# A gated recurrence on one core: loads streamed four at a time, the last two gathers first, and a reordered first layer

## The chip, the cores and the metric

The kernel runs on one core of one Trainium2 chip. The metric is the device time of one execution in microseconds (us). Three runs of the kernel before gave 105.54, 105.76 and 106.26 us, median 105.76. The profiled execution took 106.02 us; the span of its instructions, on which all times of the trace are counted, is 104.2 us.

The engines are named as the profile names them: PE (TensorE, matmul) with PEld (its weight load), DVE (VectorE), ACT (ScalarE), POOL (GpSimd) and SP (SyncE, which here only issues DMAs).

## The reference

```
state: 2048 x 256 fp32, token: 2048 int32 (49 to 31985), ih: 6 x 4000 x 256, hh: 6 x 256 x 256
for i in range(6):
    gate = ih[i][token]
    state = tanh(state + matmul(state, hh[i]) * gate)
return state
```

A token beyond the table reads its last row (row 3999). The tokens are drawn far beyond 4000, so most rows of a gather are that last row.

## The kernel before, in words

The 2048 rows lie as 16 tiles of 128 rows, handled as 8 pairs q = 0 to 7. A step is one pair in one layer, (layer, q). `order` lists the 48 steps, layer by layer, and every engine walks through that list in order with its own lag, so a step has an index i that all engines share. Work moves between engines by counting semaphores that count steps.

What one step does:
- PE, `product(i)`: state times weights. In layer 0 it is 8 fp32 matmuls from `first_cols` and `w_full` (L270). In later layers both sides are split into two fp16 halves, and a step is 12 fp16 matmuls (L278). Three PSUM banks hold products, so product(i) waits for `gated(i - 3)`.
- DVE, `gated(i)`: product times gate (L431 in layer 0, L434 later). In layer 0 it waits until both gathers of the pair have landed (`gates_in`). 
- The sum with the old state: on DVE (`add_state`, L442) in layer 0 and for the pairs of `LAST_ON_DVE` in the last layer, else on POOL (L262). `on_pool` decides.
- ACT, `new_state(i)`: tanh (L372), and for odd pairs a second tanh into PSUM (`copies`, L376).
- The new state has to be turned and split for the next layer. Even pairs: four transposes on PE (`turn`, L310, issued at step i + 3), then the first half on ACT (L354) and the rest on DVE (L448, `make_rest` at step i + 4). Odd pairs: first half on ACT (L360, at i + 1), rest on DVE (L455, `make_rest_rows` at i + 2), and then a DMA transpose issued by SP (L220).

The weights of layers 1 to 5 are split on the chip too: `w_sums` (ACT) and `scales` (DVE) find a scale, `w_make_head` (ACT, L348) makes the first half and `w_make_rest` (DVE, L419) the rest. The tables `SUMS_AT`, `TOTALS_AT`, `HEADS_AT` and `RESTS_AT` say behind which step each stands: ACT does `w_make_head` after all of its other work of that step, `new_state` included, and DVE does `w_make_rest` after its `gated` and rests. The first product of a layer (q = 0) waits for `w_rest_ready`.

Loads: `last_row` (the table's last row for every partition, 768 KB), `first_cols` (8 x 256 KB, for the layer 0 products), `state` (rows, 8 x 256 KB), and `w_full` (6 x 256 KB), all issued by SP. Before, SP issues six transfers at once (token, last row, two of `first_cols`, a weight, one of `state`), and the others as product(0) to product(5) end; the DMA transposes stand in the same queue, from i = 4 on.

Gathers (`gates`): POOL issues one indirect DMA per tile, each row 6 KB for all six layers. The tiles below `WHOLE` = 3 are gathered whole. For the others, ACT (L336) or DVE (L398) first fills the tile with the last row, and the gather then skips the rows that are out of the table. `ACT_FILLS` and `DVE_FILLS` say which engine fills which tile, and after which step (-1: before all steps). POOL issues in order of tiles, and waits for each fill.

Of the kernel before, what the change touches and what calls it, by code (L numbers as in the profile page):

```python
# [3 lines left out]


def gated_recurrence(nc, token, state_cols, state_rows, weights, gate_rows, out):

# [15 lines left out]
    VOCAB = gate_rows.shape[0] - (P - 1)  # L23
    TILES = ROWS // P
    PAIR = 2
    PAIRS = TILES // PAIR
    LAST = LAYERS - 1
    SPLIT = LAYERS - 1

    order = [(l, q) for l in range(LAYERS) for q in range(PAIRS)]  # L30
    at = {lq: i for i, lq in enumerate(order)}
    STEPS = len(order)
    END = STEPS - 1
# [7 lines left out]
    REST_LAG, REST_ROWS_LAG = 4, 2  # L41


    LAST_ON_DVE = (3, 5, 7)

    WHOLE = 3
    ACT_FILLS = {-1: (4, 7, 10), 1: (12,), 3: (14,)}
    DVE_FILLS = {-1: (3, 5, 6, 8, 9), 0: (11,), 2: (13,), 3: (15,)}  # L50


    GROUPS = ((0, 1), (1, SPLIT))
    SUMS_AT = {0: 0, 2: 1, 3: 2, 4: 3, 5: 4}
    TOTALS_AT = {3: 0, 9: 1}
    HEADS_AT = {3: 0, 12: 1, 20: 2, 28: 3, 36: 4}
    RESTS_AT = {4: 0, 13: 1, 21: 2, 29: 3, 37: 4}

    WARM = 9
    TOP = 14  # L60
    STATE_SCALE = float(2 ** 15)
    MANTISSA, BIAS = 23, 127
    INDEX_STEPS, SCALE_STEPS = 3, 4

    LOAD_LAG = 3
    PRODUCTS, TURNED, COPIES = 3, 2, 2

    def by_dma(i):
        return order[i][0] < LAST and order[i][1] in DMA_PAIRS and order[i] != LAST_TURN
# [3 lines left out]

    def on_pool(i):
        layer, q = order[i]
        return layer > 0 and not (layer == LAST and q in LAST_ON_DVE)


    def pe_turns(i):
# [2 lines left out]
    def dma_turns(i):  # L82
        return sum(by_dma(n) for n in range(i + 1))
# [11 lines left out]
    def cuts(i):  # L95
        return [slice(j, j + 1) for j in range(PAIR)] if i == END else [slice(0, PAIR)]

    with ExitStack() as ctx:
        def sb(name, shape, dt):
            return ctx.enter_context(nc.sbuf_tensor(name, shape, dt))  # L100
# [4 lines left out]
        def sem(name):  # L105
            return ctx.enter_context(nc.semaphore(name))
# [5 lines left out]
        gates = sb("gates", [P, TILES, LAYERS, HID], fp32)  # L112
# [16 lines left out]
        index = sb("index", [P, TILES], u32)  # L129
# [28 lines left out]
        product_ready = sem("product_ready")  # L158
# [10 lines left out]
        rest_rows_ready = sem("rest_rows_ready")  # L169
        stored = sem("stored")  # L170

        def pair_rows(t, q):
            return t[:, PAIR * q:PAIR * (q + 1), :]
# [13 lines left out]
        @block.sync  # L187
        def _(sp):
            def load_cols(q):
                sp.dma_start(first_cols[:, q].rearrange("p c r -> p (c r)"),  # L190
                             state_cols[q].rearrange("k c r -> k (c r)")).then_inc(cols_in[q], 16)

            def load_rows(q):
                sp.dma_start(pair_rows(state, q), pair_rows(state_rows, q)).then_inc(rows_in[q], 16)

            def load_weights(l):
                sp.dma_start(w_full[:, l], weights[l].rearrange("p c n -> p (c n)")).then_inc(w_in[l], 16)

            sp.dma_start(tok[:, :], token.rearrange("(p t) -> p t", t=TILES)).then_inc(tok_in, 16)
            sp.dma_start(last_row[:, :], gate_rows[VOCAB - 1:]).then_inc(last_in, 16)  # L200
            load_cols(0)
            load_weights(0)
            load_cols(1)
            load_rows(0)
            for i in range(STEPS):
                if i + 2 < PAIRS:
                    sp.wait_ge(product_ready, i + 1)
                    load_cols(i + 2)
                    load_rows(i + 1)
                    if i == 0:  # L210
                        load_weights(1)
                    elif i <= 2:
                        load_weights(2 * i)
                        load_weights(2 * i + 1)
                elif i + 2 == PAIRS:
                    load_rows(i + 1)
                if i >= LOAD_LAG and by_dma(i - LOAD_LAG):
                    q = order[i - LOAD_LAG][1]
                    sp.wait_ge(rest_rows_ready, dma_turns(i - LOAD_LAG))
                    sp.dma_start_transpose(split_cols[:, q].rearrange("p s j k r -> p (s j k) r"),  # L220
                                           split_rows[:, q].rearrange("p s j n -> p (s j n)")).then_inc(turned_in[q], 16)
            out_v = out.rearrange("(p t) h -> p t h", t=TILES)
            stores = 0
            for i in range(STEPS):
                layer, q = order[i]
                if layer == LAST:
                    for n, cut in enumerate(cuts(i)):
                        stores += 1
                        sp.wait_ge(state_ready, i + 1 + n)
                        sp.dma_start(pair_rows(out_v, q)[:, cut], pair_rows(state, q)[:, cut]).then_inc(stored, 16)  # L230
            sp.wait_ge(stored, 16 * stores)


        @block.gpsimd
        def _(pool):
            nc.gpsimd.iota(limit[:, :], pattern=[[0, 1]], base=VOCAB - 1, channel_multiplier=1).then_inc(limit_ready, 1)
            nc.gpsimd.memset(ident[:, :], 0.0).then_inc(ident_zero, 1)
            pool.wait_ge(ident_zero, 1)
            nc.gpsimd.affine_select(out=ident[:, :], in_=ident[:, :], compare_op=ALU.not_equal, fill=1.0,
                                    base=0, pattern=[[-1, P]], channel_multiplier=1).then_inc(ident_ready, 1)  # L240

            pool.wait_ge(index_steps, INDEX_STEPS)
            by_act = [t for tiles in ACT_FILLS.values() for t in tiles]
            by_vector = [t for tiles in DVE_FILLS.values() for t in tiles]
            for t in range(TILES):
                offset = bass.IndirectOffsetOnAxis(ap=index[:, t:t + 1], axis=0)
                row = gates[:, t].rearrange("p l h -> p (l h)")
                if t < WHOLE:
                    pool.indirect_dma_start(row, None, gate_rows, offset).then_inc(gates_in[t // PAIR], 16)
                    continue  # L250
                if t in by_act:
                    pool.wait_ge(act_filled, by_act.index(t) + 1)
                else:
                    pool.wait_ge(vector_filled, by_vector.index(t) + 1)
                pool.indirect_dma_start(row, None, gate_rows, offset, bounds_check=VOCAB - 1,  # L255
                                        oob_is_err=False).then_inc(gates_in[t // PAIR], 16)

            for i in range(STEPS):
                if on_pool(i):
                    q = order[i][1]  # L260
                    pool.wait_ge(gated_ready, i + 1)
                    nc.gpsimd.tensor_tensor(sums[:, q], sums[:, q], pair_rows(state, q),  # L262
                                            ALU.add).then_inc(pool_added, 1)
# [3 lines left out]
        def _(pe):  # L267
# [46 lines left out]
            def totals(group):  # L314
                lo, hi = GROUPS[group]
                pe.wait_ge(w_sum_ready, hi)
                nc.tensor.matmul(spare[:, 0, lo:hi], ones[:, :], w_sum[:, lo:hi],
                                 start=True, stop=True).then_inc(total_ready, 1)
# [5 lines left out]
            for i in range(STEPS):  # L324
                product(i)
                if i in TOTALS_AT:
                    totals(TOTALS_AT[i])
                if i >= TURN_LAG and by_pe(i - TURN_LAG):
# [4 lines left out]
        def _(act):  # L333
# [43 lines left out]

            for t in ACT_FILLS[-1]:
                fill(t)
            for i in range(STEPS):  # L380
# [145 lines left out]
```

## Time and profile before

| | us |
|---|---|
| median of 3 runs | 105.76 |
| profiled execution | 106.02 |
| its span | 104.2 |
| PE busy | 87.1 (84%) |
| PEld busy | 74.4 (71%) |
| DVE busy | 79.2 (76%) |
| ACT busy | 73.5 (70%) |
| POOL busy | 65.7 (63%) |

A row of the timeline gives the start in us from the start of the span, the us it takes, the engine, the line of the kernel, the operation, what it writes and reads, and the number of instructions merged in it; in brackets, how long the engine had been idle before and what ended that. Durations include the latency of an instruction, so that back-to-back instructions start closer together than they last. The chain of waits is followed back from the last instruction, and its rows are in order of time. The share of PE busy says that PE is at work most of the time, but it is an average over a start in which loads arrive and a long stretch of equal layers.

### The profile page before, as it was taken

What the parts mean: (1) busy time and instruction counts of PE and PEld (TensorE: products, weight loads), DVE (VectorE), ACT (ScalarE), POOL (GpSimd) and SP (SyncE); (2) the same over time, 40 slices, a digit from 0 to 9 for tenths busy, and PEclk for the clock granted to TensorE, in tenths of its full rate; (3) what the DMA queues carried; (4) which work ended last, traced back from release to release, by engine and by line L of the source; (5) the groups of instructions that cost most, each with busy time, mean ns of one, the idle gap of its engine ahead of it and who ended that gap; (6) DMA issues with size and microseconds to landing.
All of it is one profiled execution on the core that took longest, in us unless ns stands there. A gap on an engine that the chain in (4) does not pass through costs nothing.

```text
span 104.2 us, 1794 instructions
## 1 busy us (share of the span) xinstructions
PE 87.1 (84%) x650; PEld 74.4 (71%) x650; DVE 79.2 (76%) x127; ACT 73.5 (70%) x129; POOL 65.7 (63%) x60
## 2 busy tenths in 40 slices
PE   5919909895498998987999989999899998999900
PEld 5817608474386896976898978999789897898800
DVE  2179085283979399996979879798897978989990
ACT  4078020891897818799799996999969999667431
POOL 2687787734043008694897939979398893992440
PEclk9995885589999999999999999999999999999998
DMA  3899999999699915542387523555319654095355
GB/s 39 285 367 401 417 388 376 315 307 347 205 215 268 188 36 101 104 79 48 75 58 145 97 60 58 101 101 101 72 29 86 121 101 94 18 130 221 147 201 201
DMA packets 27128, 17.46 MB, mean 168 GB/s; under 512 B 22421, under 2 KB 22677, under 8 KB 27120
## 3 DMA queue, kind: packets, MB, share of 16 engines
q1 hardware_dynamic: 24816, 13.64, 55.2%
q0 software_dynamic: 2304, 3.71, 9.9%
q8 instruction: 5, 0.08, 0.3%
q14 instruction: 3, 0.02, 0.1%
HBM read 19.14 MB, written 2.10 MB: 204 GB/s over the span
## 4 chain that ended last, share of the span: by engine, by line
PE 51%; DMA 16%; DVE 13%; issue 9%; SPq 3%; ACT 3%; POOL 2%; POOLq 0%; DVEq 0%
PE products L278 38%; PE turned L310 7%; DMA state<-in_state_rows 6%; DVE sums L434 5%; DMA gates<-in_gate_rows,index 5%; PE products L270 5%; DMA w_full<-in_weights 5%; DVE sums L442 4%; ACT gates L336 1%; POOL sums L262 1%; DVE split_rows L455 1%; DVE split_cols L448 1%; ACT state L372 1%; SPq L190 1%; POOL gates L255 1%
## 5 line engine op out<-in xcount | busy, mean ns | idle before, releaser
L262 POOL TENSOR_TENSOR sums<-sums,state 128x512 f32<-128x512 f32 x37 | 46.8, 1274 | 21.4 <-DVE sums L434 20.5
L278 PE MATMUL products<-w_head,split_cols 128*128 128x256 f16 x316 | 54.8, 273 | 1.5 <-issue 1.5
L372 ACT ACTIVATE state<-sums 128x512 f32<-128x512 f32 (+1 forms) x49 | 30.2, 619 | 19.9 <-DVE sums L442 10.9
L278 PE MATMUL products<-w_rest,split_cols 128*128 128x256 f16 x158 | 43.1, 273 | 0.0
L278 PEld LDWEIGHTS products<-w_head,split_cols 128*128 128x128 f16 x316 | 30.9, 98 | 5.8 <-issue 2.3
L434 DVE SCALAR_TENSOR_TENSOR sums<-products,w_down,gates 128x512 f32<-128x512 f32 (+1 forms) x40 | 29.3, 735 | 0.3 <-PE products L278 0.2
L270 PE MATMUL products<-w_full,first_cols 128*128 128x256 f32 x64 | 20.1, 471 | 8.7 <-DMA first_cols<-in_state_cols 6.0
L270 PEld LDWEIGHTS products<-w_full,first_cols 128*128 128x128 f32 x64 | 14.5, 237 | 13.6 <-DMA first_cols<-in_state_cols 7.4
L255 POOL DMA_INDIRECT gates<-in_gate_rows,index x13 | 14.3, 1099 | 10.2 <-ACT gates L336 6.8
L278 PEld LDWEIGHTS products<-w_rest,split_cols 128*128 128x128 f16 x158 | 15.4, 98 | 1.7
L455 DVE SCALAR_TENSOR_TENSOR split_rows<-copies,split_rows 128x512 f16<-128x512 f32 x19 | 13.0, 686 | 3.9 <-ACT split_rows L360 3.7
L448 DVE SCALAR_TENSOR_TENSOR split_cols<-turned,split_cols 128x512 f16<-128x512 f32 x21 | 14.3, 683 | 0.3 <-ACT split_cols L354 0.2
L310 PE MATMUL turned<-ident,state 128*128 128x128 f32 x84 | 13.0, 277 | 0.7 <-ACT state L372 0.7
L354 ACT ACTIVATE split_cols<-turned 128x512 f16<-128x512 f32 x21 | 12.2, 583 | 0.0
L360 ACT ACTIVATE split_rows<-copies 128x512 f16<-128x512 f32 x19 | 11.3, 594 | 0.5
L442 DVE TENSOR_TENSOR sums<-sums,state 128x512 f32<-128x512 f32 (+1 forms) x12 | 8.9, 743 | 3.6 <-DMA state<-in_state_rows 2.4
L376 ACT ACTIVATE copies<-sums 128x512 f32<-128x512 f32 x19 | 11.2, 589 | 0.0
L310 PEld LDWEIGHTS turned<-ident,state 128*128 128x128 f32 x84 | 9.7, 143 | 2.1 <-ACT state L372 1.2
L431 DVE TENSOR_TENSOR sums<-products,gates 128x512 f32<-128x512 f32 x8 | 5.5, 688 | 7.2 <-DMA gates<-in_gate_rows,index 7.2
L336 ACT ACTIVATE gates<-last_row 128x1536 f32<-128x1536 f32 x5 | 7.2, 1471 | 3.8 <-DMA last_row<-in_gate_rows 3.8
L398 DVE COPY gates<-last_row 128x1536 f32<-128x1536 f32 x8 | 7.3, 954 | 2.8 <-DMA last_row<-in_gate_rows 2.8
L343 ACT ACTIVATE w_abs<-w_full 128x512 f32<-128x512 f32 x5 | 3.1, 619 | 3.5 <-issue 3.5
(30 smaller groups left out, 28.5 us busy)
## 6 DMA issues: line engine op xcount, KB each, us to landing
first_cols<-in_state_cols SPq DMA_DIRECT2D x8, 256.0 KB, 5.0
state<-in_state_rows SPq DMA_DIRECT2D x8, 256.0 KB, 5.9
out<-state SPq DMA_DIRECT2D x7, 256.0 KB, 2.0
w_full<-in_weights SPq DMA_DIRECT2D x6, 256.0 KB, 5.2
last_row<-in_gate_rows SPq DMA_DIRECT2D x1, 768.0 KB, 4.6
split_cols<-split_rows SPq DMA_TRANSPOSE x19, 3.1
gates<-in_gate_rows,index POOLq DMA_INDIRECT x16, 5.5
out<-state SPq DMA_DIRECT2D x2, 128.0 KB, 1.9
```

Source lines behind the costliest of these rows:

```text
L255: pool.indirect_dma_start(row, None, gate_rows, offset, bounds_check=VOCAB - 1, oob_is_err=False).then_inc(gates_in[t // PAIR], 16)
L262: nc.gpsimd.tensor_tensor(sums[:, q], sums[:, q], pair_rows(state, q), ALU.add).then_inc(pool_added, 1)
L270: last = nc.tensor.matmul(bank[:, j, :], first_cols[:, q, k, j * P:(j + 1) * P], w_full[:, 0, k * HID:(k + 1) * HID], start=(k == 0), stop ...
L278: last = nc.tensor.matmul(bank[:, j, :], split_cols[:, q, s, j, k, :], w[:, l - 1, k * HID:(k + 1) * HID], start=(n == 0), stop=(n == len( ...
L310: last = nc.tensor.transpose(turned_bank(i)[:, j, k, :], state[:, PAIR * q + j, k * P:(k + 1) * P], ident[:, :])
L354: nc.scalar.activation(split_cols[:, q, 0], turned_bank(i)[:, :, :, :], ACT.Copy, scale=STATE_SCALE).then_inc(head_ready, 1)
L360: nc.scalar.activation(split_rows[:, q, 0], copy_bank(i)[:, :, :], ACT.Copy, scale=STATE_SCALE).then_inc(head_rows_ready, 1)
L372: nc.scalar.activation(pair_rows(state, q)[:, cut], sums[:, q, cut], ACT.Tanh).then_inc(state_ready, 1)
L434: nc.vector.scalar_tensor_tensor(out=sums[:, q, cut], in0=product, scalar=down, in1=g, op0=ALU.mult, op1=ALU.mult).then_inc(gated_ready, 1)
L442: nc.vector.tensor_tensor(sums[:, q, cut], sums[:, q, cut], pair_rows(state, q)[:, cut], ALU.add).then_inc(vector_added, 1)
L448: nc.vector.scalar_tensor_tensor(out=split_cols[:, q, 1], in0=turned_bank(i)[:, :, :, :], scalar=STATE_SCALE, in1=split_cols[:, q, 0], op0 ...
L455: nc.vector.scalar_tensor_tensor(out=split_rows[:, q, 1], in0=copy_bank(i)[:, :, :], scalar=STATE_SCALE, in1=split_rows[:, q, 0], op0=ALU. ...
```

## The change

It changes five things:
- SP's loads: all 22 loads of 256 KB stand ahead of the loop, each behind the landing of an earlier one, so that about four are in flight. The transposes come behind all loads, and no load waits for a product any more.
- Gathers: the whole ones are tiles 14 and 15, and they are issued first; tiles 0 to 13 are filled and then gathered in order. ACT fills 7 tiles (5 before), DVE 7 (8 before).
- Order: steps 6 to 9 are (1, 0), (0, 6), (1, 1), (0, 7) in place of (0, 6), (0, 7), (1, 0), (1, 1).
- The sum with the old state is on DVE for steps 0 to 9 (before, 0 to 7), and in the last layer pair 6 is added to the pairs 3, 5, 7 on DVE.
- The places of the weight work: `w_make_head` and `w_make_rest` of every layer stand behind a step one later than before. Only layer 1's first product comes sooner in the list (step 6, before 8); the first products of layers 2 to 5 are steps 16, 24, 32 and 40 as before.

```diff
+    order[PAIRS - 2:PAIRS + 2] = [(1, 0), (0, PAIRS - 2), (1, 1), (0, PAIRS - 1)]
...
-    LAST_ON_DVE = (3, 5, 7)
-    WHOLE = 3
-    ACT_FILLS = {-1: (4, 7, 10), 1: (12,), 3: (14,)}
-    DVE_FILLS = {-1: (3, 5, 6, 8, 9), 0: (11,), 2: (13,), 3: (15,)}
+    POOL_FROM = PAIRS + 2
+    LAST_ON_DVE = (3, 5, 6, 7)
+    WHOLE = (14, 15)
+    ACT_FILLS = {-1: (1, 3, 5, 7), 0: (9,), 1: (11,), 2: (13,)}
+    DVE_FILLS = {-1: (0, 2, 4, 6), 0: (8, 10), 1: (12,)}
...
-    SUMS_AT = {0: 0, 2: 1, 3: 2, 4: 3, 5: 4}
-    TOTALS_AT = {3: 0, 9: 1}
-    HEADS_AT = {3: 0, 12: 1, 20: 2, 28: 3, 36: 4}
-    RESTS_AT = {4: 0, 13: 1, 21: 2, 29: 3, 37: 4}
+    SUMS_AT = {0: 0, 3: 1, 4: 2, 5: 3, 6: 4}
+    TOTALS_AT = {3: 0, 11: 1}
+    HEADS_AT = {4: 0, 13: 1, 21: 2, 29: 3, 37: 4}
+    RESTS_AT = {5: 0, 14: 1, 22: 2, 30: 3, 38: 4}
...
     def on_pool(i):
         layer, q = order[i]
-        return layer > 0 and not (layer == LAST and q in LAST_ON_DVE)
+        return i >= POOL_FROM and not (layer == LAST and q in LAST_ON_DVE)
...
             load_cols(0)
             load_weights(0)
             load_cols(1)
+            sp.wait_ge(last_in, 16)
+            load_cols(2)
+            sp.wait_ge(cols_in[0], 16)
             load_rows(0)
+            sp.wait_ge(w_in[0], 16)
+            load_weights(1)
+            sp.wait_ge(cols_in[1], 16)
+            load_cols(3)
+            sp.wait_ge(cols_in[2], 16)
+            load_rows(1)
...
+            sp.wait_ge(cols_in[5], 16)
+            load_rows(4)
...
+            sp.wait_ge(w_in[3], 16)
+            load_cols(7)
+            sp.wait_ge(cols_in[6], 16)
+            load_rows(5)
...
+            sp.wait_ge(cols_in[7], 16)
+            load_rows(7)
             for i in range(STEPS):
-                if i + 2 < PAIRS:
-                    sp.wait_ge(product_ready, i + 1)
-                    load_cols(i + 2)
-                    load_rows(i + 1)
...
-                if i >= LOAD_LAG and by_dma(i - LOAD_LAG):
+                if by_dma(i):
...
+            for t in WHOLE:
+                pool.indirect_dma_start(row(t), None, gate_rows, offset(t)).then_inc(gates_in[t // PAIR], 16)
             for t in range(TILES):
-                if t < WHOLE:
-                    pool.indirect_dma_start(row, None, gate_rows, offset).then_inc(gates_in[t // PAIR], 16)
+                if t in WHOLE:
                     continue
```

## Rows read from the trace of the kernel before

**Rows 1.** Page, the span in 40 equal slices of 2.6 us: PE busy, moved bytes.

```profile
PE   5919909895498998987999989999899998999900
GB/s 39 285 367 401 417 388 376 315 307 347 205 215 268 188 36 101 104 79 48 75 58 145 97 60 58 101 101 101 72 29 86 121 101 94 18 130 221 147 201 201
```

**Rows 2.** Chain of waits, whole span: start us, us, what (24 matmuls are two steps).

```profile
48.62 0.63 issue
49.25 2.78 PE products L278 x24
...
71.39 2.62 PE products L278 x24
74.01 0.44 PE turned L310 x4
74.44 0.28 issue
74.73 2.78 PE products L278 x24
...
87.47 2.78 PE products L278 x24
```

**Rows 3.** Timeline of PE: a warm layer 0 product, the first layer 1 matmul.

```profile
32.69 1.99 PE L270 MATMUL products<-w_full,first_cols 128*128 128x256 f32 x8 [0.45 <-DMA first_cols<-in_state_cols]
...
34.95 0.27 PE L278 MATMUL products<-w_head,split_cols 128*128 128x256 f16 x1
```

**Rows 4.** Timeline of POOL: gathers of tiles 2, 3 and 11.

```profile
5.97 1.79 POOL L249 DMA_INDIRECT gates<-in_gate_rows,index  x1 [0.30 <-issue]
8.07 1.44 POOL L255 DMA_INDIRECT gates<-in_gate_rows,index  x1 [0.30 <-issue]
...
19.61 0.99 POOL L255 DMA_INDIRECT gates<-in_gate_rows,index  x1 [0.30 <-issue]
```

**Rows 5.** The tile `gates`: its 16 gathers, from the end of the issue to landing.

```profile
DMA to landing us min/median/max: 4.4/5.5/8.2
```

**Rows 6.** Timeline of DVE, start: fills, gated(0), w_rest of layer 1, gated(7).

```profile
5.82 4.45 DVE L398 COPY gates<-last_row 128x1536 f32<-128x1536 f32 x5 [2.80 <-DMA last_row<-in_gate_rows]
13.02 0.69 DVE L431 TENSOR_TENSOR sums<-products,gates 128x512 f32<-128x512 f32 x1 [2.75 <-DMA gates<-in_gate_rows,index]
...
30.33 0.75 DVE L419 SCALAR_TENSOR_TENSOR w_rest<-w_full,w_up,w_head 128x512 f16<-128x512 f32 x1 [0.26 <-ACT w_head L348]
...
36.73 0.69 DVE L431 TENSOR_TENSOR sums<-products,gates 128x512 f32<-128x512 f32 x1 [1.95 <-DMA gates<-in_gate_rows,index]
```

**Rows 7.** Timeline of ACT at a layer's end: w_head(3), tanh(29), copies(29).

```profile
73.13 0.71 ACT L348 ACTIVATE w_head<-w_full,w_up 128x512 f16<-128x512 f32 x1
...
74.22 0.63 ACT L372 ACTIVATE state<-sums 128x512 f32<-128x512 f32 x1
74.74 0.60 ACT L376 ACTIVATE copies<-sums 128x512 f32<-128x512 f32 x1
```

**Rows 8.** Timeline of DVE at the same place: w_rest(3), then gated(30).

```profile
73.88 0.75 DVE L419 SCALAR_TENSOR_TENSOR w_rest<-w_full,w_up,w_head 128x512 f16<-128x512 f32 x1 [0.44 <-ACT w_head L348]
74.55 0.74 DVE L434 SCALAR_TENSOR_TENSOR sums<-products,w_down,gates 128x512 f32<-128x512 f32 x1
```

**Rows 9.** Timeline of POOL at the same place: the sums of steps 26 to 29.

```profile
68.41 5.17 POOL L262 TENSOR_TENSOR sums<-sums,state 128x512 f32<-128x512 f32 x4 [0.62 <-DVE sums L434]
```

**Rows 10.** Timeline of DVE in the tail, and the last sum.

```profile
99.44 1.20 DVE L442 TENSOR_TENSOR sums<-sums,state 128x256 f32<-128x256 f32 x1
...
101.06 0.42 DVE L442 TENSOR_TENSOR sums<-sums,state 128x256 f32<-128x256 f32 x1
```

**Rows 11.** Windows of PE: stretch, its us, PE busy (instructions), granted clock, DMA, GB/s.

```profile
11.46:14.87 3.41, 1.34 (x6) 1.00 1.02 403
14.87:18.28 3.41, 2.58 (x6) 0.50 1.07 379
18.28:21.70 3.42, 3.11 (x8) 0.50 0.94 315
...
25.10:28.50 3.40, 2.06 (x10) 1.00 0.72 233
```

**Rows 12.** DMA issues of the page: the DMA transposes, us to landing.

```profile
split_cols<-split_rows SPq DMA_TRANSPOSE x19, 3.1
```

More of the change, by code:

```diff
@@ L63, in gated_recurrence @@
     INDEX_STEPS, SCALE_STEPS = 3, 4
-    LOAD_LAG = 3
     PRODUCTS, TURNED, COPIES = 3, 2, 2
@@ L203, in _ @@
             load_cols(1)
+            sp.wait_ge(last_in, 16)
+            load_cols(2)
+            sp.wait_ge(cols_in[0], 16)
             load_rows(0)
-            for i in range(STEPS):
-                if i + 2 < PAIRS:
-                    sp.wait_ge(product_ready, i + 1)
-                    load_cols(i + 2)
-                    load_rows(i + 1)
[L210 to L216, printed above, removed]
-                if i >= LOAD_LAG and by_dma(i - LOAD_LAG):
-                    q = order[i - LOAD_LAG][1]
-                    sp.wait_ge(rest_rows_ready, dma_turns(i - LOAD_LAG))
+            sp.wait_ge(w_in[0], 16)
[4 more added lines that the diff above has]
+            load_rows(1)
+            sp.wait_ge(rows_in[0], 16)
+            load_cols(4)
+            sp.wait_ge(w_in[1], 16)
+            load_rows(2)
+            sp.wait_ge(cols_in[3], 16)
+            load_weights(2)
+            sp.wait_ge(rows_in[1], 16)
+            load_cols(5)
+            sp.wait_ge(cols_in[4], 16)
+            load_rows(3)
+            sp.wait_ge(rows_in[2], 16)
+            load_weights(3)
+            sp.wait_ge(w_in[2], 16)
+            load_cols(6)
+            sp.wait_ge(cols_in[5], 16)
+            load_rows(4)
+            sp.wait_ge(rows_in[3], 16)
+            load_weights(4)
+            sp.wait_ge(w_in[3], 16)
+            load_cols(7)
+            sp.wait_ge(cols_in[6], 16)
+            load_rows(5)
+            sp.wait_ge(rows_in[4], 16)
+            load_weights(5)
+            sp.wait_ge(w_in[4], 16)
+            load_rows(6)
+            sp.wait_ge(cols_in[7], 16)
+            load_rows(7)
+            for i in range(STEPS):
+                if by_dma(i):
+                    q = order[i][1]
+                    sp.wait_ge(rest_rows_ready, dma_turns(i))
                     sp.dma_start_transpose(split_cols[:, q].rearrange("p s j k r -> p (s j k) r"),
@@ L244, in _, with offset, row @@
             by_vector = [t for tiles in DVE_FILLS.values() for t in tiles]
+            def offset(t):
+                return bass.IndirectOffsetOnAxis(ap=index[:, t:t + 1], axis=0)
+            def row(t):
+                return gates[:, t].rearrange("p l h -> p (l h)")
+            for t in WHOLE:
+                pool.indirect_dma_start(row(t), None, gate_rows, offset(t)).then_inc(gates_in[t // PAIR], 16)
             for t in range(TILES):
-                offset = bass.IndirectOffsetOnAxis(ap=index[:, t:t + 1], axis=0)
-                row = gates[:, t].rearrange("p l h -> p (l h)")
-                if t < WHOLE:
-                    pool.indirect_dma_start(row, None, gate_rows, offset).then_inc(gates_in[t // PAIR], 16)
+                if t in WHOLE:
                     continue
@@ L254, in _ @@
                     pool.wait_ge(vector_filled, by_vector.index(t) + 1)
-                pool.indirect_dma_start(row, None, gate_rows, offset, bounds_check=VOCAB - 1,
+                pool.indirect_dma_start(row(t), None, gate_rows, offset(t), bounds_check=VOCAB - 1,
                                         oob_is_err=False).then_inc(gates_in[t // PAIR], 16)
```

## The prediction, made before the changed kernel was run

> **What bounds the kernel now.** I read the page's slices first [rows 1]. After the first third PE is busy in nearly every slice. Ahead of that it has gaps, while the bytes moved stand at 300 to 417 GB/s: the start belongs to transfers, the rest to PE.
>
> The chain of waits says the same [rows 2]. From 49.25 us on it is PE and nothing else: 24 matmuls (two steps) take 2.62 us, so 1.31 a step; a turn takes 0.44. A layer of eight steps and four turns is 12.24 us, and the layers begin 12.74 us apart (61.99 to 74.73, 74.73 to 87.47). The difference is mostly one short "issue" row of 0.28 ahead of each layer's first product: PE waits there for `w_rest`, which on DVE starts at 73.88 and ends just ahead of 74.73 [rows 8]. **So the second half of the weights is already on the path, by 0.3 us a layer, and whatever delays it further is paid in full.**
>
> In the start, the first layer 1 product stands at 34.95 [rows 3]. DVE walks through the layer 0 steps and waits for gathers: 2.75 us for those of pair 0 and 1.95 for those of pair 7 [rows 6].
>
> **Part 1, loads and gathers.** By the code a whole gather is 128 x 6 KB = 0.79 MB; a filled tile fetches some 16 rows of 128 (4000 of about 32000 tokens), 0.1 MB. The change has one whole gather fewer. What is moved at the start is 0.8 + 22 x 0.26 + 2 x 0.79 + 14 x 0.1 = 9.6 MB. At 376 GB/s [rows 1], from 2.3 us on, that ends at 28; at 315 GB/s at 33, and the rows of pair 5, the fourth load from the end, then land at about 29.5. Loads streamed from the start can't go much faster than the slices show already, but they no longer wait for PE.
>
> The gates then pace DVE. Tile 0 is now filled, so its gather waits for the fill: 5.82 + 0.9 = 6.7 [rows 6]. The gathers beside DVE's copies took 1.79 and 1.44 us to issue, those alone 0.99, each with 0.30 of pause [rows 4]. Tile 11, the twelfth of them, starts at 6.8 + 2 x 1.9 + 9 x 1.29 = 22.2, against 19.61 before [rows 4]. It lands 0.99 + 5.5 us later, at 28.7 (27.6 with the shortest time to landing, 31.4 with the longest) [rows 5]. The same sum puts pair 0 no sooner than the 13.02 of before [rows 6]: its gathers come behind two whole ones.
>
> What the copies do to POOL is a place where the skill speaks against the change. Rows 4 show 1.79 and 1.44 us beside the copies, so 0.8 and 0.45 more than alone. The Trainium skill (SBUF — State Buffer, "SBUF: two separate sides") says that a DVE copy of this kind locks GpSimd out of the port it writes descriptors through. If it held from the first copy to the last, tile 0 would be issued only after the fourth copy, near 9.5, and everything behind it 1.5 us later. The trace does not agree with so long a lock: a gather begun at 5.97 ended at 7.76, with copies running to 10.27. The sum goes by rows.
>
> **Part 2, the first layer 1 product.** It needs `w_rest` of layer 1, which stands on DVE behind step 5. After the gates of pair 5 DVE does gated(5), a rest, a sum and `w_rest`, about 0.6 to 0.67 from start to start each [rows 6, 8]: 2.5 us, so 28.7 + 2.5 = **31.2** (30.1 to 33.9). That is 3.75 us sooner than 34.95. But two layer 0 products (1.8 each warm, [rows 3]) and one turn (0.44) now come behind it, 4.0 us in all. Nothing is won: the same work is merely in another order.
>
> **Part 3, from there to step 16.** PE: 8 x 1.31 + 2 x 1.8 + 5 x 0.44 = 16.3 us. Before, the stretch from 34.95 to 49.25 was 14.3 for 12.2 us of work, so 2.1 of waits. After, (0, 7) gets its DMA transpose (3.1 us to landing [rows 12]) from step 9 and needs it at step 15, six steps instead of eight: I take 1.0 us of wait. `w_rest` of layer 2 brings the wait of part 4, 1.2; small ones 0.4. The sum is 18.9, so step 16 starts at 50.1 against 49.25: **+0.85** (47.5 to 53.4, so -1.75 to +4.15). Steps 8 and 9 put their sums on DVE in place of POOL, 0.6 each; DVE has room, since PE takes 3.1 us for a layer 0 and a layer 1 product together and a step costs DVE about 1.8. SP's transposes now stand behind all loads. The one of pair 1 can go at about 28 and is needed at step 8, past 34; hidden. If the loads ran to 33, step 8 would wait 1 to 2 us.
>
> **Part 4, the weight work one step later.** Before, ACT did w_head(3) behind tanh(28), at 73.13, and only then head(26), tanh(29) at 74.22 and copies(29) at 74.74 [rows 7]. After, w_head(3) stands behind tanh(29) and copies(29). Tanh(29) can't start ahead of POOL's sum of step 29, which ends at 68.41 + 5.17 = 73.58 [rows 9]. So tanh 73.6, copies 74.1, w_head 74.7 to 75.4, w_rest 75.5 to 76.2, first product 76.3 against 74.73: 1.6 later. With engines that have caught up during the stall, the chain is counted from the end of product 29 at 71.39 - 0.44 = 70.95: gated 0.74, POOL 1.28, tanh 0.52, copies 0.6, w_head 0.71, w_rest 0.75, 4.6 us without hand-offs, where PE has 3.5 us of work (two steps, two turns). That stalls it 1.1 to 1.2 in place of 0.28. I take **0.9 more** a layer, nearest to the caught-up case, since every stall lets them catch up; three layers (24, 32, 40) are **+2.7** (0 to +4.8). Nothing covers it: PE can't go on to a step behind in its list.
>
> **Part 5, tail and clock.** The half sum at 99.44 took 1.20 beside a POOL sum, and 0.42 alone [rows 10]. With pair 6 on DVE that is -0.8, and a full sum of 0.6 is added: **-0.2** (-0.8 to +0.6). Clock: PE was 1.34 of 3.41 us busy in one window and had 0.50 (1.2 of 2.4 GHz) for the next two, while 2.06 busy kept 1.00 [rows 11]. After the change PE finishes product 5 near 25 and waits until 31.2, nearly idle, so it may start layer 1 at half speed. The loss is nothing or up to half of 6.8 us, and part of it hides behind the waits of part 3. I take **+0.5** (0 to +3.4). The Trainium skill (TensorE: Matmul & The Clock Gate, "What's actually happening") says that an idle engine falls to half rate and comes back after sustained activity; by that the full term would be due, and it is a rival below.
>
> **Sum:** 0.85 + 2.7 - 0.2 + 0.5 = +3.85. Against the profiled execution (106.02, its span 104.2) it is a span of 108.05 and 109.9; the median is 0.26 below the profiled one, so **109.6 us**.
>
> **Rivals.** About 1% is what can be told from no change.
> - *Faster.* The start wins and the late weights cost nothing: gathers land in the shortest time (part 2 at 30.1), the waits of part 3 shrink to 1.1, and the stall at a layer's end is covered because ACT runs less behind. -1.75 + 0 - 0.2 gives 103.8. For it: loads wait for nothing. Against: rows 7 to 9. It decides if the extra stall is under 0.3 a layer. Chance 0.18.
> - *No change.* The same good start with 0.7 a layer: -1.75 + 2.1 - 0.2 = +0.15, 105.9. Chance 0.12.
> - *Slower at the start.* PE goes half speed into layer 1, or loads and gathers together run at 315 GB/s and pair 5 comes at the long end. With the clock's loss at 3.4 instead of 0.5 the sum is +6.75, 112.5; with part 2 at 33.9, +6.55. For it: the window of 1.34 us [rows 11]. Against: such waits partly hide each other. Chance 0.13.
> - *The streaming does nothing*, since the DMA was full already. The gates pace the start in any case, so this gives the forecast's time and is part of it.
>
> The forecast has 0.57. Slower 0.70, same 0.12, faster 0.18. The range is 104.9 to 112.4: it leaves out the better half of the faster case and the worst end of the last. The likeliest case's own range is 107.3 to 111.5.
>
> **What would show it.** The gather of tile 11 starts near 22; gated(5) waits for a gather and stands near 28.7; the first fp16 product near 31; step 16 near 50. In the chain of waits, the issue rows ahead of steps 24, 32 and 40 grow from 0.28 to about 1.2, and layers start 13.6 us apart, with w_rest waiting for w_head. The clock's windows between 28 and 38 tell the clock term. If layers still start 12.7 apart, part 4 is wrong, and the kernel is not slower; if the first fp16 product stands at 28 or sooner, part 1 is.

## The result

The changed kernel takes 111.36 us (median of 4 runs, 110.63 to 111.81), the kernel before 105.78 in the same comparison: ratio 1.0515, 95% interval [1.0443, 1.0587]. It is slower by 5%. The profiled execution took 111.81 us, its span is 110.0 us. The forecast was 109.6 us, in a range of 104.9 to 112.4.

| place on the span, us | before | forecast | after |
|---|---|---|---|
| gather of tile 11 issued | 19.61 | 22.2 | 23.46 |
| gated(5) | 31.00 | 28.7 | 28.58 |
| first fp16 product | 34.95 | 31.2 | 31.24 |
| step 16 (layer 2) | 49.25 | 50.1 (50.6 with the clock) | 52.37 |
| from layer to layer | 12.74 | 13.6 | 13.71 |
| step 40 to the end of the span | 16.73 | 16.5 | 16.49 |
| span | 104.2 | 108.05 | 110.0 |

The kernel before was run again beside each group of experiments and scattered more there than in the first runs, so that the ratios below carry wider intervals. Executions disturbed by a slower state of the chip are left out of the ratios; the profiled ones of experiments 2 and 7 are among them, so that their places and spans stand in brackets and are not set against the others, and experiment 7 has one execution left, too few for a ratio.

The page of the changed kernel, slices of 2.75 us, PE busy and granted clock. Against the slices of before [rows 1] the hole has moved: PE is idle in the tenth and eleventh slice (24.75 to 30.25 us), and right behind it the clock stands at half for two slices.

```profile
PE   6929936890069999975999959999599995999910
...
PEclk9996799999855999999999999999999999999996
```

The chain of waits of the changed kernel. Against [rows 2] it has an issue row of 1.3 to 1.4 us ahead of the first product of layers 2 to 5, where there were 0.28 and 0.63. At the start, the first fp16 product (12 matmuls of step 6) takes 2.72 us instead of 1.31, and the layer 0 product behind it 2.90.

```profile
27.24 4.00 issue
31.24 2.72 PE products L313 x12
33.95 2.90 PE products L305 x8
...
45.94 3.03 DMA split_cols<-split_rows
...
49.02 1.48 PE products L313 x12
50.50 0.44 PE turned L345 x4
50.94 1.43 issue
52.37 2.78 PE products L313 x24
...
64.76 1.32 issue
66.08 2.78 PE products L313 x24
...
78.47 1.33 issue
79.81 2.78 PE products L313 x24
...
92.19 1.32 issue
93.51 2.78 PE products L313 x24
```

Windows of PE around the hole, changed kernel (stretch, its us, PE busy and instructions, granted clock, DMA share, GB/s). PE does nothing for a whole stretch, at first still at clock 1.00, and is at 0.50 (1.2 of 2.4 GHz) when layer 1 starts. The clock of [rows 11] fell in the same way, behind a stretch in which PE did little.

```profile
25.10:28.50 3.40, 0.00 (x0) 1.00 0.99 327
28.50:31.90 3.40, 0.66 (x4) 0.63 1.05 218
31.90:35.00 3.10, 3.10 (x13) 0.50 0.42 84
```

Timeline of DVE, changed kernel. Gated(0) waits 6.07 us for its gathers (2.75 in [rows 6]); gated(5) waits for a gather and stands where the forecast had it; `w_rest` of layer 1 is behind it; and at a layer's end `w_rest` waits 0.84 for `w_head` and stands at 78.95, 0.86 ahead of the product that needs it.

```profile
15.61 0.69 DVE L466 TENSOR_TENSOR sums<-products,gates 128x512 f32<-128x512 f32 x1 [6.07 <-DMA gates<-in_gate_rows,index]
...
28.58 0.69 DVE L466 TENSOR_TENSOR sums<-products,gates 128x512 f32<-128x512 f32 x1 [0.76 <-DMA gates<-in_gate_rows,index]
...
30.39 0.75 DVE L454 SCALAR_TENSOR_TENSOR w_rest<-w_full,w_up,w_head 128x512 f16<-128x512 f32 x1
...
78.95 0.75 DVE L454 SCALAR_TENSOR_TENSOR w_rest<-w_full,w_up,w_head 128x512 f16<-128x512 f32 x1 [0.84 <-ACT w_head L383]
```

Timeline of ACT at the same layer's end. Tanh(29) waits for POOL's sum, `copies` comes next, and only then `w_head`: the order that the prediction wrote from [rows 7].

```profile
77.15 0.63 ACT L407 ACTIVATE state<-sums 128x512 f32<-128x512 f32 x1 [0.19 <-POOL sums L297]
77.69 0.58 ACT L411 ACTIVATE copies<-sums 128x512 f32<-128x512 f32 x1
78.21 0.71 ACT L383 ACTIVATE w_head<-w_full,w_up 128x512 f16<-128x512 f32 x1
```

### The profile page after: what moved, and what is told of

The parts are those of the page before. It is cut to its first block, busy times and chain, and to the rows that moved or that the text cites. A ratio compares the mean times of both kernels' runs of the same rounds, so it can differ in the third digit from the quotient of the medians.

```text
span 110.0 us, 1796 instructions
## 1 busy us (share of the span) xinstructions
PE 85.8 (78%) x650; PEld 74.4 (68%) x650; DVE 80.2 (73%) x129; ACT 76.7 (70%) x131; POOL 61.3 (56%) x57
## 4 chain that ended last, share of the span: by engine, by line
PE 51%; DMA 18%; DVE 12%; issue 11%; ACT 5%; POOL 0%; SPq 0%; POOLq 0%; DVEq 0%
PE products L313 40%; DMA gates<-in_gate_rows,index 11%; PE turned L345 7%; DVE sums L469 5%; DMA last_row<-in_gate_rows 4%; PE products L305 4%; ACT gates L371 4%; DVE sums L477 4%; DMA split_cols<-split_rows 3%; DVE split_cols L483 2%; DVE split_rows L490 1%; ACT state L407 1%; DVE sums L466 1%; POOL gates L290 0%; SPq L201 0%
## 5 line engine op out<-in xcount | busy, mean ns | idle before, releaser
L313 PE MATMUL products<-w_head,split_cols 128*128 128x256 f16 x316 | 56.5, 276 | 12.8 <-issue 12.1
L297 POOL TENSOR_TENSOR sums<-sums,state 128x512 f32<-128x512 f32 x34 | 43.1, 1270 | 33.6 <-DVE sums L469 33.3
L313 PE MATMUL products<-w_rest,split_cols 128*128 128x256 f16 x158 | 43.6, 276 | 0.0
L305 PE MATMUL products<-w_full,first_cols 128*128 128x256 f32 x64 | 17.8, 437 | 4.0 <-DMA w_full<-in_weights 2.2
L290 POOL DMA_INDIRECT gates<-in_gate_rows,index x14 | 15.4, 1099 | 6.0 <-issue 3.4
L305 PEld LDWEIGHTS products<-w_full,first_cols 128*128 128x128 f32 x64 | 13.8, 224 | 7.1 <-issue 4.6
L371 ACT ACTIVATE gates<-last_row 128x1536 f32<-128x1536 f32 x7 | 10.0, 1470 | 3.9 <-DMA last_row<-in_gate_rows 3.9
L477 DVE TENSOR_TENSOR sums<-sums,state 128x512 f32<-128x512 f32 (+1 forms) x15 | 10.2, 679 | 0.3
L433 DVE COPY gates<-last_row 128x1536 f32<-128x1536 f32 x7 | 6.4, 962 | 2.9 <-DMA last_row<-in_gate_rows 2.9
L454 DVE SCALAR_TENSOR_TENSOR w_rest<-w_full,w_up,w_head 128x512 f16<-128x512 f32 x5 | 3.8, 751 | 3.7 <-ACT w_head L383 3.7
```

The source lines that it names most:

```text
L290: pool.indirect_dma_start(row(t), None, gate_rows, offset(t), bounds_check=VOCAB - 1, oob_is_err=False).then_inc(gates_in[t // PAIR], 16)
L305: last = nc.tensor.matmul(bank[:, j, :], first_cols[:, q, k, j * P:(j + 1) * P], w_full[:, 0, k * HID:(k + 1) * HID], start=(k == 0), stop ...
L313: last = nc.tensor.matmul(bank[:, j, :], split_cols[:, q, s, j, k, :], w[:, l - 1, k * HID:(k + 1) * HID], start=(n == 0), stop=(n == len( ...
L371: nc.scalar.activation(gates[:, t].rearrange("p l h -> p (l h)"), last_row[:, :], ACT.Copy).then_inc(act_filled, 1)
L477: nc.vector.tensor_tensor(sums[:, q, cut], sums[:, q, cut], pair_rows(state, q)[:, cut], ALU.add).then_inc(vector_added, 1)
```

## The experiments

| | kernel | ratio to before, 95% interval | first fp16 product | step 16 | span |
|---|---|---|---|---|---|
| | before | 1 | 34.95 | 49.25 | 104.2 |
| | changed | 1.0515 [1.0443, 1.0587] | 31.24 | 52.37 | 110.0 |
| 1 | changed, weight work back | 1.0103 [1.0058, 1.0148] | 31.16 | 50.54 | 105.0 |
| 2 | before, weight work late | 1.0419 [1.0313, 1.0524] | | (52.77) | (110.6) |
| 3 | changed, PE kept warm | 1.0439 [1.0354, 1.0525] | 31.04 | 49.75 | 107.4 |
| 11 | changed, both | 0.9962 [0.9849, 1.0075] | 31.39 | 48.67 | 103.1 |
| 9 | as 1, layer 1's weight work sooner too | 0.9839 [0.9741, 0.9937] | 29.00 | 47.67 | 102.1 |
| 5 | loads and gathers, old order | 0.9758 [0.9671, 0.9845] | 30.18 | 46.15 | 101.1 |
| 6 | new order alone | 0.9889 [0.9781, 0.9997] | 30.85 | 48.31 | 102.4 |
| 7 | streamed loads alone | none; 105.89 beside 106.04 | (32.86) | (52.32) | (106.8) |
| 8 | new gathers alone | 0.9784 [0.9682, 0.9886] | 34.60 | 47.00 | 101.7 |
| 10 | as 5, tiles 0 and 1 whole | 0.9541 [0.9388, 0.9694] | | 43.89 | 98.7 |
| 12 | as 10, pair 6 summed on DVE | 0.9688 [0.9630, 0.9746] | | 45.60 | 100.1 |
| 4 | before, weight work sooner | 1.0027 [0.9982, 1.0071] | | | 104.6 |

### 1 and 2. The late weight work, undone and done alone

```diff
-    HEADS_AT = {4: 0, 13: 1, 21: 2, 29: 3, 37: 4}
-    RESTS_AT = {5: 0, 14: 1, 22: 2, 30: 3, 38: 4}
+    HEADS_AT = {4: 0, 12: 1, 20: 2, 28: 3, 36: 4}
+    RESTS_AT = {5: 0, 13: 1, 21: 2, 29: 3, 37: 4}
```

> The changed kernel, with the weight work of layers 2 to 5 back behind the steps it had before (w_head at 12, 20, 28, 36, w_rest one later). Theory (the late weight work is what stalls PE ahead of each layer): the layers start about 12.8 us apart instead of 13.7, the issue rows ahead of steps 24, 32 and 40 fall from 1.3 to about 0.3, and with the one ahead of step 16 (1.43) the time falls by 3.0 to 4.0 us, to about 107.5 to 108.5. Rival (the longer layers come from the new lag of the engines, or from the order of the start): the layers stay over 13.4 apart and the time falls by less than 1 us.

Measured: 4.1% less than the changed kernel's ratio, 4.4 us. In its chain of waits the issue rows are 0.19 to 0.29 again, and the layers start 12.75 apart (62.95, 75.70, 88.44). Nothing is left ahead of step 16.

```profile
50.10 0.44 PE turned L345 x4
50.54 2.62 PE products L313 x24
...
75.40 0.29 issue
75.70 2.78 PE products L313 x24
```

The opposite edit, on the kernel before:

```diff
-    HEADS_AT = {3: 0, 12: 1, 20: 2, 28: 3, 36: 4}
-    RESTS_AT = {4: 0, 13: 1, 21: 2, 29: 3, 37: 4}
+    HEADS_AT = {3: 0, 13: 1, 21: 2, 29: 3, 37: 4}
+    RESTS_AT = {4: 0, 14: 1, 22: 2, 30: 3, 38: 4}
```

> The kernel before, with the weight work of layers 2 to 5 one step later, as in the changed kernel, and nothing else. Theory: four stalls grow by about 0.9 to 1.0 each, the time rises by 3.0 to 4.0 us, to about 109 to 109.8, and the layers start 13.7 apart. Rival: in the old start ACT runs further behind, so that the late place costs more than 1.3 a layer (over +5), or the stall is given back in the tail (under +1.5).

Measured: +4.2%, 4.4 us, [3.3, 5.6]. Four issue rows of 1.33, and layers 13.72 apart (52.77, 66.49, 80.21, 93.92): the stall does not depend on how the kernel starts. By these rows it is 4 x 1.33 against 0.63 + 3 x 0.28, so 3.85 us.

```profile
51.44 1.33 issue
52.77 2.78 PE products L278 x24
```

The two edits agree in size, from both sides. **The late weight work of layers 2 to 5 is the largest part of the loss, about 4 us.** Experiment 9 takes up the late place of layer 1's.

### 3 and 11. PE kept warm through the hole

```diff
             for i in range(STEPS):
+                if order[i] == (1, 0):
+                    pe.wait_ge(gated_ready, i + 1 - PRODUCTS)
+                    for _ in range(26):
+                        nc.tensor.matmul(products[i % PRODUCTS][:, 0, 0:P], ones[:, :], ones[:, :], start=True, stop=True)
                 product(i)
```

> The changed kernel, with 26 matmuls of ones into an unused bank between PE's last work of step 5 and the first layer 1 product, which overwrites them. They fill most of the 6.7 us in which PE idles. Theory (PE goes into layer 1 at 0.5 because it idled): the granted clock stays 1.00 to step 10, the products of steps 6 and 7 take 1.3 and 1.8 us instead of 2.7 and 2.9, and the time falls by 1.5 to 2.6 us. Rival (DVE and the DMA transposes bound the stretch up to step 16 anyway): the two products are faster but step 16 starts where it did, within 0.5 us, and the time stays.

Measured: the stretches of PE show the clock at 1.00 throughout. The first fp16 product starts at 31.04, as without them (31.24), and step 16 at 49.75 instead of 52.37, 2.6 us sooner; the stalls at the layers' ends stay (1.33).

```profile
28.50:31.90 3.40, 2.59 (x24) 1.00 1.19 208
31.90:35.00 3.10, 3.10 (x23) 1.00 0.65 129
```

The timed gain is smaller and not clear: 1.0439 against 1.0515, 0.8 us, with intervals that overlap. So I put the same matmuls on top of experiment 1.

> The changed kernel with both: the 26 matmuls that keep PE busy, and the weight work of layers 2 to 5 back. If the two terms are independent, the span is 105.0 - 2.6 = 102.4 and the time about 104 us; if the warm clock only uncovers another wait ahead of step 16 (the DMA transpose of pair 7), it is 105.5 to 106.5.

Measured: step 16 at 48.67 against 50.54 without them, 1.9 us sooner, span 103.1 against 105.0; ratio 0.9962 against 1.0103, 1.4%, intervals just overlapping. Two traces say 2.6 and 1.9, two timings 0.8 and 1.5. By these four numbers the half clock costs 0.8 to 2.6 us, in a place that leads to the end; neither timing is clear of its interval. The spans add up nearly as if the terms were independent (102.4 expected, 103.1 found); the times less so, since the executions that count took 105.19 to 106.12 where about 104 was expected.

### 9. Layer 1's weight work where it was

```diff
-    HEADS_AT = {4: 0, 12: 1, 20: 2, 28: 3, 36: 4}
-    RESTS_AT = {5: 0, 13: 1, 21: 2, 29: 3, 37: 4}
+    HEADS_AT = {3: 0, 12: 1, 20: 2, 28: 3, 36: 4}
+    RESTS_AT = {4: 0, 13: 1, 21: 2, 29: 3, 37: 4}
```

> The changed kernel with the weight work of layers 2 to 5 back, and layer 1's w_head behind step 3 and w_rest behind step 4, as before. Theory (PE idles 6.7 us only because w_rest of layer 1 stands behind gated(5), which waits for a gather): the first layer 1 product starts at about 28.5 instead of 31.2, PE idles about 4 us, and the time is 1.5 to 4 us under that of the kernel with the weight work back alone (1.010 of before), so about 103 to 105. Rival (the stretch up to step 16 is bound by the gathers of pairs 6 and 7 and by the DMA transpose of pair 7): the first product is sooner, step 16 is not, and the time stays near 106.5 to 107.

Measured: first fp16 product at 29.00, step 16 at 47.67 against 50.54 in experiment 1, ratio 0.9839 against 1.0103: 2.6% less. This one index, `w_rest` of layer 1 behind step 5 in place of 4, put the wait for the gathers of pair 5 ahead of the whole of layer 1. Of the 2.87 us at step 16, 2.16 are there at the first product already (31.16 to 29.00). Layer 1 also starts at full clock here: its first product takes 1.31 us and the layer 0 product behind it 1.73, where experiment 1 has 2.72 and 2.57; most of that is given back in the wait that comes next (18.67 us from there to step 16, 19.38 in experiment 1). So this 2.6% is not to be added to what experiments 3 and 11 say of the half clock. The wait is seen in its chain: the DMA transpose of pair 1, which SP issues only behind all loads (27.14), is needed at step 8 and lands 6.65 us later; PE idles 1.20 us for it.

```profile
27.14 6.65 DMA split_cols<-split_rows
...
33.84 1.48 PE products L313 x12
```

### 5 to 8. The parts of the start, one by one

Experiment 5 is the changed kernel without the new order, and with the places of the weight work and of the sums as before:

```diff
-    order[PAIRS - 2:PAIRS + 2] = [(1, 0), (0, PAIRS - 2), (1, 1), (0, PAIRS - 1)]
...
-    POOL_FROM = PAIRS + 2
-    LAST_ON_DVE = (3, 5, 6, 7)
+    POOL_FROM = PAIRS
+    LAST_ON_DVE = (3, 5, 7)
...
-    SUMS_AT = {0: 0, 3: 1, 4: 2, 5: 3, 6: 4}
-    TOTALS_AT = {3: 0, 11: 1}
-    HEADS_AT = {4: 0, 13: 1, 21: 2, 29: 3, 37: 4}
-    RESTS_AT = {5: 0, 14: 1, 22: 2, 30: 3, 38: 4}
+    SUMS_AT = {0: 0, 2: 1, 3: 2, 4: 3, 5: 4}
+    TOTALS_AT = {3: 0, 9: 1}
+    HEADS_AT = {3: 0, 12: 1, 20: 2, 28: 3, 36: 4}
+    RESTS_AT = {4: 0, 13: 1, 21: 2, 29: 3, 37: 4}
```

> The changed kernel with the old order of steps, the old places of the weight work and the old split of the sums between DVE and POOL; left of the change are the streamed loads and the new gathers and fills. Theory (what the new order wins it pays back as PE work behind it, so the start alone decides): the gathers land as in the changed kernel, pair 5 near 28.5 and pair 7 near 12, the first layer 1 product starts near 35, as before, and the time is within 1 us of before. Rival (the streamed start is a gain that the order loses): the first layer 1 product starts at 33 or sooner and the time is 1.5 us or more below before.

The rival held, against my theory: 0.9758, and the first fp16 product at 30.18. The timeline of PE shows why. The products of pairs 6 and 7 run at 24.59 and 26.84, in the very stretch in which PE of the changed kernel has nothing to do, since they need only their loads and the bank that gated(3) or gated(4) frees. In the changed kernel the same two stand in PE's list behind (1, 0), which waits for `w_rest`. But experiment 5 differs from the changed kernel in the weight work too, also in layer 1's `w_rest`, which stands behind step 4. Experiment 9 has that place with the new order, so it is the nearer comparison for the order: step 16 at 47.67 there against 46.15 here, ratios 0.9839 and 0.9758 with intervals that overlap. The order costs 1.5 us on these two traces, and the times do not settle it.

```profile
24.59 1.89 PE L305 MATMUL products<-w_full,first_cols 128*128 128x256 f32 x8
26.84 2.00 PE L305 MATMUL products<-w_full,first_cols 128*128 128x256 f32 x8 [0.35 <-DMA first_cols<-in_state_cols]
29.69 0.66 PE L345 MATMUL turned<-ident,state 128*128 128x128 f32 x4 [0.86 <-ACT state L407]
30.18 0.27 PE L313 MATMUL products<-w_head,split_cols 128*128 128x256 f16 x1
```

Experiments 6, 7 and 8 put one part each on the kernel before: the line of `order` (6), the list of loads on SP (7), and the tables of fills with `WHOLE = (14, 15)` and their order on POOL (8), all as in the diff of the change.

> The kernel before with the new order of the eight to ten steps alone: (1, 0), (0, 6), (1, 1), (0, 7) at steps 6 to 9. Loads, gathers, weight work and the places of the sums stay. Theory (the order costs by the DMA transpose of (0, 7), needed at step 15 and no longer at 17 steps' distance of eight, and by nothing else): the first layer 1 product comes near 31, a wait of about 1 us stands ahead of step 15 or 17, and the time is 0 to 1.5 us above before. Rival (starting layer 1 sooner gives PE work while pairs 6 and 7 are still loading): 1 us or more below before.

Measured: 0.9889, the interval ends at 0.9997, so a small gain: its estimate of 1.2 us is what the rival asked for, its interval reaches from nothing to 2.3. With late loads of pairs 6 and 7, layer 1 does have something to do sooner (first fp16 product at 30.85, no half clock). The DMA transpose of (0, 7) is the wait that was expected: step 15 stands right behind its landing.

```profile
43.30 3.04 DMA split_cols<-split_rows
...
46.39 1.48 PE products L279 x12
```

> The kernel before with the streamed loads alone; gathers, fills and order stay. Theory (the gates pace DVE in the start, and the loads were near what the DMAs can move): the products of layer 0 run ahead, gated still waits for the gathers of pairs 0 to 2, the gathers land a little later than before because they share the DMAs with loads, and the time is within 1 us of before. Rival (loads were late in the start): sums no longer wait for state rows, and the time is 1.5 us or more below before.

Measured: no ratio. The one execution that counts took 105.89, beside a median of 106.04 for the kernel before: neither a gain nor a loss is shown. The rows of the profiled execution say nothing of the time, but show a wait that a streamed start can run into: the first DMA transpose is issued at 30.94, behind all loads, and lands 7.74 us later; step 9 waits 4.39 us for it, and PE goes on at half clock.

```profile
30.94 7.74 DMA split_cols<-split_rows
...
38.73 2.74 PE products L305 x12
```

> The kernel before with the new gathers and fills alone (tiles 14 and 15 whole and first); loads and order stay as before. With the streamed loads alone and both together in the old order, this closes a square of four. Theory (each alone leaves one late: the loads alone make the gathers of pairs 6 and 7 collide with the first DMA transposes, the gathers alone leave the loads behind PE's products): the time is within 1.5 us of before, and only both together give 2.6 us. Rival (the gathers alone are the gain): 2 us or more below before.

Measured: 0.9784, the rival: the gathers alone carry the gain that experiment 5 has. The last two gathers are issued at 25.07 and 26.36 instead of 29.86 and 31.24 (gated(7) waited for them to 36.73 [rows 6]); they are now those of pair 6, and pair 7's, the whole ones, come first. Streaming on top moves the point estimate by 0.3%, less than the intervals.

### 10 and 12. A better version

```diff
-    WHOLE = (14, 15)
-    ACT_FILLS = {-1: (1, 3, 5, 7), 0: (9,), 1: (11,), 2: (13,)}
-    DVE_FILLS = {-1: (0, 2, 4, 6), 0: (8, 10), 1: (12,)}
+    WHOLE = (0, 1)
+    ACT_FILLS = {-1: (3, 5, 7, 9), 0: (11,), 1: (13,), 2: (15,)}
+    DVE_FILLS = {-1: (2, 4, 6, 8), 0: (10, 12), 1: (14,)}
```

> The loads-and-gathers version in the old order, with tiles 0 and 1 gathered whole and first in place of 14 and 15 (ACT fills 3, 5, 7, 9, then 11, 13, 15; DVE 2, 4, 6, 8, then 10, 12, 14). Every filled gather moves up by two places in POOL's queue, and pair 0 does not wait behind somebody else's whole tiles. Theory (the gathers pace DVE in the start): gated(0) at about 13 instead of 15.9, the gather of tile 11 about 2.6 us sooner, step 16 1 to 2.5 us sooner, and the time about 101 to 102.5. Rival (loads or the DMA transposes bound the start by then): gated(0) is sooner, the time stays near 103.

Measured, on top of experiment 5: 0.9541, span 98.7. Gated(0) stands at 12.46 (15.86 in experiment 5, 15.61 in the changed kernel).

```profile
12.46 0.69 DVE L466 TENSOR_TENSOR sums<-products,gates 128x512 f32<-128x512 f32 x1 [3.08 <-DMA gates<-in_gate_rows,index]
```

Experiment 12 adds pair 6 to `LAST_ON_DVE`, as the change had it.

> The version with tiles 0 and 1 whole and first, streamed loads and the old order, with pair 6 of the last layer also summed on DVE. Theory (this part of the change is worth 0.2 us by the rows of the tail, 16.49 us from step 40 to the end against 16.73): from the start of step 40 to the end of the span it takes 16.4 to 16.6 us, where the version without it took 16.8, and the time is 100.5 to 103. Rival: DVE's extra sum delays the last ones and the tail is 16.9 or longer. The ratio to before, measured in more rounds, also says again what the first pair's whole gathers are worth: under 0.965 if that result holds.

Measured: 0.9688 [0.9630, 0.9746], median 102.37 beside 105.98. That does not reach the "under 0.965" which I had asked of it: the gain over before is sure, its size is 3 to 4%, and with intervals of 0.9541 and 0.9758 that this one overlaps, what the whole first pair adds to experiment 5 is not settled by times. The tail takes 100.1 - 83.55 = 16.55 us against 98.7 - 81.92 = 16.78 without: the 0.2 us of the theory. The profiled execution starts its layers later than that of experiment 10, and its chain shows by what: the first DMA transpose, issued behind the last loads, landed at 34.29 here and at 32.48 there.

```profile
28.42 5.87 DMA split_cols<-split_rows
...
34.33 1.48 PE products L313 x12
```

### 4. The weight work sooner than in the kernel before

```diff
-    HEADS_AT = {3: 0, 12: 1, 20: 2, 28: 3, 36: 4}
-    RESTS_AT = {4: 0, 13: 1, 21: 2, 29: 3, 37: 4}
+    HEADS_AT = {3: 0, 10: 1, 18: 2, 26: 3, 34: 4}
+    RESTS_AT = {4: 0, 11: 1, 19: 2, 27: 3, 35: 4}
```

> The kernel before, with the weight work of layers 2 to 5 two steps sooner (w_head at 10, 18, 26, 34, w_rest one later). Theory: the four issue rows of 0.28 to 0.63 ahead of steps 16, 24, 32 and 40 go away, and the time falls by 0.8 to 1.3 us, to about 104.7. Rival: the same work of ACT and DVE only delays something else by as much (a head or rest of a state), and the time is the same within 0.3 us.

Measured: 1.0027, no difference: the rival. The issue row ahead of each layer is gone, but a turn now waits 0.3 to 0.45 us for its tanh, and the chain no longer runs through PE: it goes round DVE, POOL and ACT, with `w_head` and `w_rest` in it.

```profile
83.25 0.62 ACT w_head L348
83.87 0.02 issue
83.89 0.75 DVE w_rest L419
84.64 0.67 DVE sums L434
...
85.39 2.54 POOL sums L262 x2
```

So the 0.28 us a layer of before could not be had by moving the weight work sooner; by this chain the loop of the other engines is as long as PE's.

## Why the prediction was right, and where it was not

The direction, the mechanism and most places were right; the size was 1.95 us short on the span (+3.85 said, +5.8 measured). Term by term:

**Part 4, the weight work: right.** +2.7 said for three layers, +2.92 measured (93.51 - 52.37 against 87.47 - 49.25). The chain counted from gated to `w_rest` gave a stall of 1.1 to 1.2 with engines that had caught up; it is 1.32. Experiments 1 and 2 show it from both sides.

**Part 2, the first fp16 product: the place right, the conclusion wrong.** It stands at 31.24 for 31.2 said, by the luck of part 1, below. But the sentence "Nothing is won: the same work is merely in another order" compared with the kernel before, whose layer 0 products are also late. Against its own loads the changed start loses: experiment 5 has its first fp16 product at 30.18, with both layer 0 products done. Most of that loss is the place of layer 1's `w_rest`, and less, if anything, the order (experiment 9 against 1 and 5). That a product which needs only a load can fill a stretch in which everything else waits for `w_rest` was in the code, in the three PSUM banks, and I had even written that PE would idle from 25 to 31.2. I did not ask which work could have stood there.

**Part 1: right by luck, three errors that cancel.** The gather of tile 11 was issued 1.3 us later than said. It landed 5.0 us after the start of its issue, at 28.5, where I took the median of 5.5. And I had added 0.99 for the issue itself, although the view counts from the start of the issue and not from its end, as the caption of [rows 5] has it: a gather's row in the chain of waits begins where POOL's does (20.48 in both) and ends at the landing. The same view of the changed kernel:

```profile
DMA to landing us min/median/max: 4.2/5.0/7.7
```

The 1.3 us have two sources. The first filled gather began at 7.67, not at 6.8, though its fill ended at 6.87, with the first of DVE's four copies. And two later gathers, of tiles 7 and 9, took 1.70 and 1.35 us to issue where the sum had 0.99; both stood beside copies of DVE (16.95 to 18.77, 20.01 to 20.96), and the sum had slowed only the first two gathers for that. Timelines of DVE and POOL, changed kernel:

```profile
5.91 3.63 DVE L433 COPY gates<-last_row 128x1536 f32<-128x1536 f32 x4 [2.90 <-DMA last_row<-in_gate_rows]
7.67 1.11 POOL L290 DMA_INDIRECT gates<-in_gate_rows,index  x1 [2.01 <-ACT gates L371]
...
23.46 0.99 POOL L290 DMA_INDIRECT gates<-in_gate_rows,index  x1 [0.30 <-issue]
```

The 0.80 us from the fill to the gather are not the copies' doing. In the kernel before, a gather that waits for a fill of ACT starts as late behind it (27.60 + 1.47 = 29.07, gather at 29.86), and DVE copies nothing then:

```profile
27.60 1.47 ACT L336 ACTIVATE gates<-last_row 128x1536 f32<-128x1536 f32 x1
29.86 1.08 POOL L255 DMA_INDIRECT gates<-in_gate_rows,index  x1 [4.93 <-ACT gates L336]
```

So on the port rule of the Trainium skill (SBUF — State Buffer, "SBUF: two separate sides") the trace says that no gather waited here for a run of copies, which ended at 9.54; what is left for the rule is that gathers take longer to issue beside copies (1.11 to 1.70 us in the changed kernel, 0.99 alone). The sum of moved bytes is 9.5 MB and not 9.6, which moves nothing.

That pair 0 would wait behind the whole tiles was said, but given no price. The prediction's own terms would have had it (tile 1 starts at 6.8 + 1.9, and 1.6 + 5.5 more give 15.8); gated(0) started at 15.61 instead of 13.02.

**Part 3: nearly right.** From the first fp16 product to step 16 it said 18.9 us. With the clock held, experiment 3 takes 49.75 - 31.04 = 18.71. The transpose of (0, 7) cost 0.7 to 0.9 of the 1.0 said, and the wait ahead of step 16 was 1.2 to 1.4.

**Part 5: the tail right, the clock mis-sized.** The tail gave 0.24 for 0.2 said. "I take +0.5" for the half clock was the step that failed: the stretch took 21.13 us where 18.71 do with the clock held, so 2.4 us on this trace. The two slow products cost 1.4 and 1.2 us, and nothing hid them, since the waits behind them (a transpose, `w_rest`) hang on work that PE itself had delayed. The Trainium skill (TensorE: Matmul & The Clock Gate, "What's actually happening") would have had the full term: an idle engine falls to half rate. The trace agrees with it here, with 0.50 after a stretch of 0.00 busy, and I had weighed it down without a row that spoke for doing so. The full term was 3.4 by the prediction's bound; the timings of experiments 3 and 11 say 0.8 and 1.5, so how far 0.5 was off in the median time is less sure than on the trace.

**The rivals.** "The streaming does nothing" is not contradicted: the one execution of experiment 7 that counts is level with before, and on top of the new gathers the step is within the intervals (5 against 8). But the reason given, that gates pace the start in any case, hid that the new gathers are worth 2.2% by themselves. The faster rival's starting half was there, then, and it was lost inside the change. The ratios give the steps from the changed kernel back: 1.0515; 1.0103 with the weight work of layers 2 to 5 back (1); 0.9839 with layer 1's back too (9); 0.9758 with the old order and the old places of the sums (5). All but the last 0.8% of that is the place of the weight work. The likeliest case's own range, 107.3 to 111.5, has no sum behind it; the measured 111.36 lies just inside.

What stays open: how much of experiment 10's lead over 5 is real, what the order costs by itself, and why the first transpose takes 4.4 to 7.7 us to land in the start. That it shares the DMAs with loads and gathers is only argued. Where it stands between the loads it took 4.4 and 4.7 (experiments 6 and 8), and with all loads ahead of it 4.5 to 7.7.

## What to carry to other kernels

An instruction in an in-order list may be moved only so far as the work queued ahead of it has landed: one index later put `w_rest` behind a gather, and another put `w_head` behind a tanh and a copy, 1 us a layer. When PE is predicted to idle, ask what in its list could run there, and price the half clock behind the idle in full. And take a change of several parts apart before judging it: here the gathers were a gain of 2% that the other parts, the late weight work above all, turned into a loss of 5%.

## What the runs showed of the hardware

PE idle for 6.7 us came back at clock 0.50 and stayed there for about 5 us of full work (31.24 to about 36.2, slices of 1.00 behind it); with 26 matmuls of no use in that gap it stayed at 1.00. A DMA transpose that takes 3.0 us later in the kernel took 6.65 and 7.74 us in the start, issued while loads and gathers were in flight. A gather that waited for its fill started 0.79 to 0.80 us after the fill's end, with DVE's copies beside it (6.87 to 7.67) and without (29.07 to 29.86).
